# Two graph layers on one core: two looped layer programs against one unrolled program with a hand-drawn memory map

## What is computed

```python
h = jnp.einsum('bnd,ade->bane', feat_in, W)          # layer 0
th = jnp.tanh(h)
attn = (th @ w_src) + swapaxes(th @ w_dst)
attn = softmax(where(mask, -999.0, leaky(attn)))
feat_out = elu(attn @ h + b)
gate = sigmoid(feat_in @ H_w.T + H_b)
x = layernorm(x + gate * feat_out + (1 - gate) * x)
q, k, v = x @ Wq + bq, x @ Wk + bk, x @ Wv + bv      # layer 1
probs = softmax(q k^T / sqrt(128) + bias(adj))
x = layernorm(x + (probs @ v) @ Wf + bf)
```

## Time and profile before

| | us |
|---|---|
| median of 3 runs | 2995.43 |
| profiled execution | 2993.85 |
| its span, first to last instruction | 2992.1 |
| PE busy | 2876.0 |
| DVE busy | 1720.1 |
| ACT busy | 1061.4 |
| POOL busy | 471.6 |

### The profile page before, as it was taken

The page is one execution under the profiler, slowest core; times in us unless marked ns, Lnnn a source line. Parts: engine busy times, 40 slices in busy tenths (PEclk is TensorE's granted clock), DMA queues, the critical chain, the costliest instruction groups (busy, mean ns, idle before and its releaser), DMA issues.

```text
span 2992.1 us, 55247 instructions
## 1 busy us (share of the span) xinstructions
PE 2876.0 (96%) x21696; PEld 2654.9 (89%) x21696; DVE 1720.1 (57%) x3335; ACT 1061.4 (35%) x2597; POOL 471.6 (16%) x265
## 2 busy tenths in 40 slices
PE   7999999999999619999999999999999999999998
PEld 6888888888888519999999999999999999999998
DVE  6888888888888644444444444444444444444443
ACT  4554445445454423322232232233223222322332
POOL 0111111110111011111211211121111112111110
PEclk9999999999999859999999999999999999999999
DMA  4332332233323241111111211111121111111110
GB/s 149 103 99 99 103 106 98 98 101 106 106 95 101 101 159 54 54 44 65 65 43 45 75 54 44 65 56 52 44 66 63 43 55 64 54 44 65 64 33 22
DMA packets 107364, 221.15 MB, mean 74 GB/s; under 512 B 36544, under 2 KB 36544, under 8 KB 107200
## 3 DMA queue, kind: packets, MB, share of 16 engines
q1 hardware_dynamic: 107200, 218.58, 21.9%
HBM read 142.65 MB, written 75.89 MB: 73 GB/s over the span
## 4 chain that ended last, share of the span: by engine, by line
PE 62%; DMA 1%; DVE 1%; issue 0%; POOL 0%; ACT 0%; SPq 0%; DVEq 0%; POOLq 0%
PE L_ps_k L108 14%; PE L_ps_q L108 14%; PE L_ps_a L108 14%; PE L_ps_a L957 14%; PE L_ps_s L920 2%; PE L_ps_c L940 2%; PE L_ps_pt L940 1%; PE L_ps_pt L927 1%; PE L_ps_q L871 0%; PE L_ps_s L871 0%; PE L_ps_k L871 0%; DMA L_gate<-gate_scratch 0%; DMA L_x_tok<-Wf 0%; DMA L_x_tok<-Wk 0%; DVE L_w_lo L97 0%
## 5 line engine op out<-in xcount | busy, mean ns | idle before, releaser
L424 PE MATMUL L_ps_hg<-L_w_hi,L_xT_hi 128*128 128x512 f32 x1152 | 474.0, 411 | 11.7 <-DVE L_w_lo L97 11.4
L424 PE MATMUL L_ps_hg<-L_w_hi,L_xT_lo 128*128 128x512 f32 x1152 | 455.9, 396 | 0.0
L424 PE MATMUL L_ps_hg<-L_w_lo,L_xT_hi 128*128 128x512 f32 x1152 | 455.9, 396 | 0.0
L108 PE MATMUL L_ps_q<-L_xT_hi,L_w_hi 128*128 128x256 f32 x1152 | 328.2, 285 | 7.4 <-issue 6.0
L108 PE MATMUL L_ps_k<-L_xT_hi,L_w_hi 128*128 128x256 f32 x1152 | 332.5, 289 | 0.0
L108 PE MATMUL L_ps_q<-L_xT_lo,L_w_hi 128*128 128x256 f32 x1152 | 326.7, 284 | 0.0
L108 PE MATMUL L_ps_q<-L_xT_hi,L_w_lo 128*128 128x256 f32 x1152 | 326.6, 284 | 0.0
L108 PE MATMUL L_ps_k<-L_xT_hi,L_w_lo 128*128 128x256 f32 x1152 | 325.8, 283 | 0.0
L108 PE MATMUL L_ps_k<-L_xT_lo,L_w_hi 128*128 128x256 f32 x1152 | 325.6, 283 | 0.0
L657 ACT ACTIVATE L_qT<-L_ps_q,L_bq_col 128x256 f32<-128x256 f32 x192 | 80.5, 470 | 687.9 <-PE L_ps_q L108 687.9
L424 PEld LDWEIGHTS L_ps_hg<-L_w_hi,L_xT_hi 128*128 128x128 f32 x1152 | 217.3, 189 | 61.2 <-DVE L_w_lo L97 9.2
(11 more groups left out here) (110 smaller groups left out, 5939.6 us busy)
## 6 DMA issues: line engine op xcount, KB each, us to landing
L_x_tok<-x SPq DMA_DIRECT2D x64, 384.0 KB, 3.3
L_dst_all<-dst_scratch SPq DMA_DIRECT2D x128, 192.0 KB, 3.3
gate_scratch<-L_gate SPq DMA_DIRECT2D x64, 384.0 KB, 2.5
feat_scratch<-L_feat SPq DMA_DIRECT2D x64, 384.0 KB, 2.3
L_x_tok<-x SPq DMA_DIRECT2D x32, 768.0 KB, 4.3
L_feat<-feat_scratch SPq DMA_DIRECT2D x64, 384.0 KB, 3.1
L_gate<-gate_scratch SPq DMA_DIRECT2D x64, 384.0 KB, 3.6
out<-L_x_tok SPq DMA_DIRECT2D x32, 768.0 KB, 3.5
```

What stands on the lines that cost most here:

```text
L108: ins = pe.matmul(out, left[a][c], right[b][c], start=(n == 0), stop=(n == len(terms) - 1))
L424: ins = pe.matmul(ps_hg[:, cols], xT[a][c], w[bb][c], start=(c == 0 and n == 0), stop=(c == KC - 1 and n == 2))
```

## The change

Both layers become one program, `two_graph_layers`, without a loop: all 64 tiles and 32 groups are written out, and every count that is waited for is a constant. Parts that fell away are `split_weights`, `steps`, `groups` and the two unroll constants.

All SBUF tiles get hand-drawn addresses. The region of `Wq` and `Wk` (hi and lo) is free of layer 0's tiles. `Wv` and `Wf` share the region of layer 0's weights. The first group's feat and gate (`feat_first`, `gate_first`) lie for a while where `Wq` goes later. A raw chunk is loaded into the place of its `lo` part and replaced there, so there is no stage with slots. To make room, layer 0's `x_tok`, `feat` and `gate` get one buffer each, `probs` is `logits`, and `th_dst` is `dst_all`. Layer 1's small tiles overlie layer 0's.

What moves:

- At the start, SP issues `x` of tile 0, six chunks of `W0`, two of adj, six chunks of `H_t`, four constant rows, and then `x` of tile 1 behind a wait for `xT_done`.
- After step 5, x, feat and gate of group 0 are loaded; POOL and DVE mix and normalise them in steps 6 to 11.
- In steps 14 to 26 one chunk a step of `Wq` and `Wk` is loaded and split.
- After the last `project(2)`, the 12 chunks of `Wv` and `Wf` are loaded; their split is spread over the last tiles' work and group 0.
- PE transposes group 0's x right after the transposes of tile 62's probabilities; the attention of tiles 62 and 63 and the transposes of tile 63's probabilities lie between the queries and keys of group 0.
- In layer 1, `out` is stored tile by tile.

```diff
-LAYER0_UNROLL = 4
-LAYER1_UNROLL = 2
...
+        MAT = KC * D * 4
+        wq_hi, wq_lo, wk_hi, wk_lo = (at(n * MAT, name, [P, KC, D], F32R)
+                                      for n, name in enumerate(("wq_hi", "wq_lo", "wk_hi", "wk_lo")))
+        w0_hi = at(4 * MAT, "w0_hi", [P, KC, 2 * D], F32R)
+        w0_lo = at(6 * MAT, "w0_lo", [P, KC, 2 * D], F32R)
+        wv_hi, wv_lo, wf_hi, wf_lo = (at((4 + n) * MAT, name, [P, KC, D], F32R)
+                                      for n, name in enumerate(("wv_hi", "wv_lo", "wf_hi", "wf_lo")))
+        w0_raw = at(6 * MAT, "w0_raw", [P, KC, 2 * D])
...
+        th_dst = dst_all
+        logits = at(S + 33792, "logits", [P, D])
+        probs = logits
...
+            load_x(0)
+            for n in range(KC):
+                load_chunk(sp, w0_chunks[n], w0_in[n])
+            for T in range(2):
+                load_adj(T)
+            for n in range(KC, 2 * KC):
+                load_chunk(sp, w0_chunks[n], w0_in[n])
+            for out_, row in ((wdst_all, w_dst), (wsrc_all, w_src), (b_less1, b0), (Hb_less1, H_b)):
+                sp.dma_start(out_[:, :], row.partition_broadcast(P)).then_inc(consts_in, 16)
+            sp.wait_ge(xT_done, 1)
+            load_x(1)
...
+            sp.wait_ge(g_done, NT)
+            for n in range(EARLY_W1, 4 * KC):
+                load_chunk(sp, w1_chunks[n], w1_in[n])
+            store_gate(NT - 1)
+            store_feat(NT - 2)
...
+                for t in range(GT):
+                    sp.wait_ge(norm_done, GT * G + t + 1)
+                    sp.dma_start(out_g[G][:, t, :], x1_tok[s][:, t, :]).then_inc(stored[s], 16)
...
+            def softmax_scores(T):
+                dve.wait_ge(dst_in, 32 * (T + 1))
+                dve.wait_ge(src_done, T + 1)
+                if T >= 1:
+                    dve.wait_ge(pt_done, T)
...
+            def values(T):
+                pe.wait_ge(ident_ok, 1)
+                pe.wait_ge(ptc_done, T + 1)
+                if T >= 1:
+                    pe.wait_ge(att_done, T)
...
+            for T in range(NT):
+                pe.wait_ge(lo_done, T + 1)
+                if T >= 1:
+                    pe.wait_ge(h_copied, T)
+                project(0, T)
+                if T + 1 < NT:
+                    transpose_x(T + 1)
+                if T >= 1:
+                    pe.wait_ge(z_done, T)
+                project(1, T).then_inc(h_done, 1)
+                if T >= 2:
+                    values(T - 2)
+                project(2, T).then_inc(g_done, 1)
+                if T >= 1:
+                    transpose_probs(T - 1)
...
+            pe.wait_ge(w1_ready, EARLY_W1)
+            transpose_x1(0)
+            for G in range(NG):
+                pe.wait_ge(x1lo_done, 3 * (G + 1))
                 query(G, 0)
+                if G == 0:
+                    values(NT - 2)
                 key(G, 0)
+                if G == 0:
+                    transpose_probs(NT - 1)
                 query(G, 1)
+                if G == 0:
+                    values(NT - 1)
+                    pe.wait_ge(z_done, NT)
                 scores(G, 0)
```

More of the change, by code:

```diff
@@ L141, in layer0 @@
[L141 to L152, removed]
@@ L197, in steps @@
[L197 to L210 removed]
+        z_done, gate_done, feat_stored, gate_stored = (
+            sem(n) for n in ("z_done", "gate_done", "feat_stored", "gate_stored"))
@@ L245, in _, with load_x, load_adj, store_gate @@
-            steps(sp, step, NT + 2)
+            def load_x(T):
+                sp.dma_start(x_tok[:, :], x_t[T]).then_inc(x_in, 16)
+            def load_adj(T):
+                sp.dma_start(adj_u8[:, T % 4, :], adj_t[T]).then_inc(adj_in[T % 4], 16)
+            def store_gate(T):
+                sp.wait_ge(gate_done, 2 * (T + 1))
+                sp.dma_start(gate_t[T], gate[:, :]).then_inc(gate_stored, 16)
+            def store_feat(T):
+                sp.wait_ge(elu_done, T + 1)
+                sp.dma_start(feat_t[T], feat[:, :]).then_inc(feat_stored, 16)
@@ new lines, in _ @@
+            round_x1(0)
+            copy_probs(NT - 2)
+            gate_of(NT - 1)
+            act.wait_ge(cols_in, 48)
+            act.wait_ge(thsrc_done, NT)
+            q_out(0, 0)
+            bias_of_mask(0)
+            exp_scores(NT - 1)
+            for n in range(3):
+                w1_round(act, EARLY_W1 + n)
+            k_out(0, 0)
+            elu_exp(NT - 2)
+            copy_probs(NT - 1)
+            for n in range(3, KC):
+                w1_round(act, EARLY_W1 + n)
+            for G in range(NG):
+                if G >= 1:
+                    bias_of_mask(G)
+                    q_out(G, 0)
+                    k_out(G, 0)
@@ new lines, in project @@
+            def project(k, T):
+                cols = slice(k * BLK, (k + 1) * BLK)
+                left = [[xT[:, T % 2, part, c, :] for c in range(KC)] for part in range(2)]
+                right = [[t[:, c, cols] for c in range(KC)] for t in (w0_hi, w0_lo)]
+                for c in range(KC):
+                    if T == 0:
+                        pe.wait_ge(w0_ready, (0 if k == 0 else KC) + c + 1)
+                    for n, (a, b) in enumerate(((0, 0), (0, 1), (1, 0))):
+                        ins = pe.matmul(ps_hg[:, cols], left[a][c], right[b][c], start=(c == 0 and n == 0),
+                                        stop=(c == KC - 1 and n == 2))
+                return ins
```

1208 lines of the change are left out of this document (593 added, 615 removed).

## The result

| | before | after |
|---|---|---|
| median | 2995.61 us (4 runs) | 2882.2 us (2880.14 to 2889.13, 4 runs) |
| ratio, 95% interval | | 0.9626 (0.9609 to 0.9643) |
| profiled execution | 2993.85 | 2889.13 |
| its span | 2992.1 | 2887.4 |

The change takes off 113 us. The profiled execution of after is the longest of its four.

The account below looks back on a forecast made before the run. PE's own work was taken to bound the steady parts; border 85, loops 9, start 3 and tail 1 made 98 off the profiled 2993.85, 2895.9, or 2897 as median, with an 8 in 10 range of 2887 to 2920.

Parts of the forecast that it names:

- The walk through the border: Between the layers: the new order placed on the old timeline, query 0 at about 1021.1, output 0 near 1074.1.
- (a): Group 0: tile 63's late elu delays head pair 1's exponentials, and roundings hold PE's third scores; 1.5 us uncovered.
- (b): Group 0: group 1's second mix, moments and norm lie together on DVE before `x1_ready`; 0.7 us late.
- (c): Group 0: three rests of 0.96 stand before `output(0, 0)`, which waits for all 24 chunks; 1.3 us late.
- the term of 85: Border: group 1's output starts at 1132.2 instead of 1217.11, a gain of 85 us (78 to 88).
- `Wq` and `Wk` cost nothing: Layer 0: 12 steps each take one more ACT rounding and one more DVE rest, which fit in idle time; 0 us.
- The loops, 9: Layer 1: 13 branches cost 0.7 us each, so writing the loop out gains 9; layer 0 gains nothing.
- The start, 3: Start: x of tile 1 lands at 20.9 and step 1 begins at 31.5 instead of 34.67; gain 3 us (-3.5 to 4.5).
- Groups 58.14 apart: Layer 1: a sign that the forecast is right, all groups staying 58.14 us apart, the old spacing without a branch.
- The half open border: Rival, chance 0.13: splits of `Wv` and `Wf` fall on PE's path in group 0, 22.6 us come back, 2920.
- Streaming: Rival, chance 0.05: in layer 0 each block of 256 instructions costs 0.7 us, 40 us in all, 2937.
- DVE became a bound: Rival, chance 0.02: in layer 0 DVE is delayed by shared buffers, PE waits each step, slower than before at 3004.

Follow-up runs that it names:

- `a_align0`: The kernel after with its small tiles moved by 96 bytes, so that x of both layers lies at multiples of 128 bytes; 2900.71 us, ratio 0.9692.
- `a_pool`: The kernel after, with POOL in group 0 waiting for all 24 chunks before it adds the bias bf to x; 2881.15 us, ratio 0.9626.
- `b_unroll`: The kernel before with both loops written out and nothing else changed; 2984.17 us, ratio 0.9969.
- `b_unroll_pad32`: The kernel before with both loops written out and layer 1's x_hi and x_lo 32 bytes beyond a multiple of 128; 2968.61 us, ratio 0.991.
- third program: No kernel: only matmul bursts on zeros at the kernels' addresses, operands shifted up to 224 bytes; layer 0's burst took 227.1 ns a matmul at 0, 232.2 at 128.
- first program: No kernel: only bursts of 36 matmuls on zeros, varying where both operands begin; at 256 columns 4.31 us with both at 0, 4.08 with the streamed one 64 further.
- `a_x1_pool`: The kernel after with x of tile 1 loaded ahead of `H_t` and POOL waiting for all 24 chunks in group 0; 2870.69 us, ratio 0.9594.

## Why the prediction came out as it did

- *What bounds the kernel, and where a change can win.* Right for the four places named. Wrong in what followed from it, that PE's own work in the steady parts is a constant. It shrank by 20 us on the page, and by 6 in `a_align0`.
- *The walk through the border.* Forecast: query 0 at 1021.1 after some 2 us of idle PE; it came at 1020.77 after 1.78. Tile 63's elu on DVE, behind `q_out(0, 2)`, did hold the scores of head pair 1. Output 0 was forecast at 1074.1 and came at 1078.67.
- *The stalls of group 0.* They were forecast as (a) 1.5, (b) 0.7 and (c) 1.3, in sum 3.5. PE idled 1.0 before the third scores, 3.42 for the norm of group 1's second x, and 2.45 for the last rest, 6.9 in all. So (a) was too large and (b) and (c) too small, since their VectorE operations were priced from rows in which POOL rests ("three rests of 0.96", a mix of about 1): beside POOL three rests took 5.93 and the mix 2.58. A sign of the forecast failed with them: the granted clock did not stay at 1.00 through the border (0.96 in 1022 to 1080 us). It fell to 0.50 after each of the two long waits, which the sum had no term for; outputs of group 0 took 1.4 us longer than those of other groups, and from query 0 to output 0 PE needed 1.6 us more, its waits left out, than in `a_pool` at full clock. With POOL out of the way the three waits are 0.95, 1.32 and 0.85, the clock stays at 1.00, and output 0 starts 62.31 us after attention 61; forecast were 1074.1 - 1011.12 = 62.98. So without that contention the walk is right to 0.7 us, 3.1 us of waits against 3.5, though each of the three is off by about half a us and they cancel in part, and the term of 85 was 3 to 6 too large by the contention between VectorE and POOL, which the prediction did not look for. The Trainium skill (SBUF — State Buffer, Who interferes with whom) says that a VectorE instruction with both inputs in SBUF contends with a GpSimd instruction that reads SBUF. The trace agrees: the rests (5.93 against 2.68) and the mix (2.58 against 0.95) are slowed, while `bn_stats` with its one input (1.02 in both places) is not.
- *`Wq` and `Wk` cost nothing; added waits cost nothing.* Right. Layer 0's 61 steps take 954.18 us against 952.95. The 1.2 more go with the address: with x moved by 96 bytes to where it lay within 256 (`a_align0`) they take 951.15, less than before the change.
- *The loops, 9.* Right in both halves. 9.2 by the run that wrote them out, all in layer 1, none in layer 0. The prediction set beside it a rule of the Trainium skill (Runtime: NRT & Kernel Launch, Instruction fetch mechanics) that would give 9 more in layer 0. The page states the stall for a taken branch whose target is not among the pages already fetched, and that condition was left out. The 3 packets in 500 us say that layer 0's loop was not fetched anew, and nothing was to be gained: 952.98 us against 952.95 for the 61 steps of `b_unroll`. By the counts of the earlier trace rows the body of that loop has 912 matmuls and weight loads, the body of layer 1's loop some 1790, with 138 packets. That the length of the body decides is not tested.
- *The start, 3.* 1.3: PE's transposes of x of tile 1 begin at 21.63, where 20.9 was forecast, and after the gap PE ran at half clock until 27.5, for 5.9 us where 3 were assumed.
- *The tail, 1.* 0.6 to 0.8.
- *Groups 58.14 apart.* This is the step that failed. The prediction named it as a sign ("all groups 58.14 apart") and gave no term and no bound for it, in the sum or in the range. The groups are 57.5 to 57.6 apart because the new memory map has moved layer 1's tiles: it puts x 32 bytes beyond the place of its weights within 256 bytes, where before they began at the same place, and 36 matmuls of a query take 4.20 us instead of 4.32. With x back at a multiple of 128 (`a_align0`) the time is 2900.7, 4 above the forecast and inside the range; the pad of 32 bytes alone, in the kernel before, brings 14.5 us. The other 1.5 to 5.4 us of the pace go with the outputs, 12.84 us in `b_unroll_pad32` and 12.67 or 12.88 in after; what chooses between these two is open. The diff had it in plain sight: a hand-drawn map changes every address.
- *The range.* Its lower end, 2887, is not what its own ends add up to. No stalls (3.5 less) and the best start (1.5 less) lead from 2897 to 2892; no term stands for the other 5 us. The measured 2882.2 lies 10 below the sum of the good ends.
- *The rivals.* The half open border shows its place rightly (output 0 waits for a rest of `Wf`), but with 2.45 us of idle PE, not 22.6 in all. Streaming costs nothing in layer 0: 29 packets in 500 us in `b_unroll` too, and its steps are as long as before. No gap named after `h_copied` or the transposes shows that DVE became a bound; that the border would stay was far off.

## What to carry to other kernels

When a change moves tiles, the price of each steady matmul is a term of the sum with bounds of its own: here a pad of 32 or 128 bytes moved the time by 14 to 16 us of 2993. Before pricing waits, compare where both operands of the steady matmuls begin in the two kernels, and test it by a pad that nothing reads. A duration taken from a row holds only with the same neighbours: look what POOL does at the place where a VectorE operation is put.

## What the runs showed of the hardware

- The pace of fp32r matmuls with a weight load each depends on where the two operands begin relative to each other within 256 bytes. In the third program, 512 columns at the same place take 227 ns a matmul, with 32 to 160 or 224 bytes between 232 to 234, with 192 229. 256 columns take 119.9 at the same place and with 96 bytes, and 117.8 to 118.7 at the other multiples of 32. For 384 the values reach from 173.3 to 177.8. The difference alone does not fix the pace: in the first program 256 columns took 113.4 with 64 bytes between and 117.9 with both moved by 32. The Trainium skill (TensorE: Matmul & The Clock Gate, Step-by-step: what each phase is for) says that the weight load has a read port of its own and takes nothing from the running matmul. These runs show a dependence on both addresses, of up to 8% between the fastest and the slowest burst of 256 columns (113.4 and 122.9). Whether it is the two reads that meet is not shown.
- The 72 output matmuls of a group took either 12.66 or 12.88 us at the same addresses: by turns in the first profile of after, three times in 32 in its second, never in `a_x1_pool`. The cause is open.
- VectorE operations with two inputs in SBUF took 2.2 to 3.4 times as long beside POOL's operations on two tiles (three rests 5.93 against 2.68, a multiplication of 256 columns 1.42 against 0.42), and POOL's pair of additions took 4.54 instead of 3.66. How much they meet differs between executions (rests of 5.93 and 4.32 in the same kernel).
